# A fused LoRA feed-forward kernel: the first step rebuilt around a table that is split on the chip

## What is computed

```
def _lora_linear(x, W, A, B, adapter_indices):
    base = jnp.einsum('bsd,df->bsf', x, W)
    Ai = A[adapter_indices]
    Bi = B[adapter_indices]
    lora = jnp.einsum('bsr,brf->bsf', jnp.einsum('bsd,bdr->bsr', x, Ai), Bi)
    return base + lora
gate = _lora_linear(x, Wg, Ag, Bg, adapter_indices)
up = _lora_linear(x, Wu, Au, Bu, adapter_indices)
h = jax.nn.silu(gate) * up
x = x + _lora_linear(h, Wd, Ad, Bd, adapter_indices)
w = weights[subjects]                      # subjects: the same numbers
x = x + jnp.einsum('bct,bcd->bdt', x, w)
```

## Time and profile before

| | us |
|---|---|
| median of three runs (1300.89 to 1303.17) | 1301.45 |
| profiled execution | 1302.31 |
| its span | 1300.7 |
| TensorE busy | 1216.8 (94%) |
| VectorE busy | 781.4 (60%) |
| ScalarE busy | 525.4 (40%) |
| GpSimd busy | 94.9 (7%) |

### The profile page before, as it was taken

The page is one execution under the profiler, slowest core; times in us unless marked ns, Lnnn a source line. Parts: engine busy times, 40 slices in busy tenths (PEclk is TensorE's granted clock), DMA queues, the critical chain, the costliest instruction groups (busy, mean ns, idle before and its releaser), DMA issues.

```text
span 1300.7 us, 22988 instructions
## 1 busy us (share of the span) xinstructions
PE 1216.8 (94%) x7104; PEld 1083.9 (83%) x7104; DVE 781.4 (60%) x1389; ACT 525.4 (40%) x999; POOL 94.9 (7%) x188
## 2 busy tenths in 40 slices
PE   3656999989999989999999999998999999999998
PEld 2545778878888878888878888888999999999997
DVE  4534666786667776667777667754444554445453
ACT  2423444454444454344454444434333333334332
POOL 1200110000110000000000000010112111211110
PEclk9777999999999989999999999998999999999999
DMA  3346776477665566757656777656555545554540
GB/s 140 106 144 220 196 211 201 140 207 213 183 180 163 153 187 202 200 151 190 169 160 180 196 212 208 188 167 190 147 168 175 153 142 163 177 151 148 160 131 36
DMA packets 114492, 221.33 MB, mean 170 GB/s; under 512 B 26434, under 2 KB 68546, under 8 KB 114370
## 3 DMA queue, kind: packets, MB, share of 16 engines
q1 hardware_dynamic: 106112, 198.80, 53.0%
q0 software_dynamic: 7392, 19.41, 4.7%
q10 hardware_dynamic: 866, 1.66, 0.3%
HBM read 173.62 MB, written 46.14 MB: 169 GB/s over the span
## 4 chain that ended last, share of the span: by engine, by line
PE 80%; SPq 7%; DVE 4%; issue 3%; DMA 3%; ACT 2%; DVEq 0%; ACTq 0%
PE ps L894 14%; PE ps L895 14%; PE ps L896 13%; PE ps L906 8%; PE ps L1005 5%; PE ps L1009 5%; PE ps L1013 4%; PE ps L1012 4%; PE ps L1007 4%; PE ps L1014 4%; SPq L201 4%; PE ps L923 1%; ACT xo_hi L370 1%; SPq L159 1%; DMA bq<-b_dram 1%
## 5 line engine op out<-in xcount | busy, mean ns | idle before, releaser
L894 PE MATMUL ps<-xo_hi,w_hi 128*128 128x512 f32 x896 | 360.8, 403 | 29.2 <-DVE v L684 13.4
L895 PE MATMUL ps<-xo_lo,w_hi 128*128 128x512 f32 x896 | 356.2, 398 | 0.0
L896 PE MATMUL ps<-xo_hi,w_lo 128*128 128x512 f32 x896 | 353.2, 394 | 0.0
L894 PEld LDWEIGHTS ps<-xo_hi,w_hi 128*128 128x128 f32 x896 | 171.8, 192 | 62.1 <-DVE v L684 16.1
L896 PEld LDWEIGHTS ps<-xo_hi,w_lo 128*128 128x128 f32 x896 | 171.2, 191 | 38.4
L906 PEld LDWEIGHTS ps<-t_st,bq 128*128 128x128 f32 x1024 | 158.1, 191 | 51.2 <-DMA bq<-b_dram 30.9
L895 PEld LDWEIGHTS ps<-xo_lo,w_hi 128*128 128x128 f32 x896 | 171.9, 192 | 26.6
L906 PE MATMUL ps<-t_st,bq 128*128 128x256 f32 x1024 | 165.0, 284 | 28.5 <-DMA bq<-b_dram 28.5
L604 DVE TENSOR_TENSOR w_lo<-wsum,w_hi 128x512 fp32r<-128x512 f32 x128 | 88.5, 692 | 143.7 <-ACT w_hi L370 143.7
L604 DVE TENSOR_TENSOR hl<-h_raw,hh 128x1024 fp32r<-128x1024 f32 x64 | 78.4, 1225 | 158.6 <-ACT hh L370 158.5
L1005 PE MATMUL ps<-wd_hl,hh 128*128 128x320 f32 x512 | 161.5, 315 | 7.5 <-DVE hl L604 4.8
(11 more groups left out here) (73 smaller groups left out, 1559.5 us busy)
## 6 DMA issues: line engine op xcount, KB each, us to landing
bq<-b_dram SPq DMA_DIRECT2D x1024, 64.0 KB, 2.2
raw<-packed SPq DMA_DIRECT2D x64, 512.0 KB, 5.4
h_dram<-h_f SPq DMA_DIRECT2D x64, 512.0 KB, 3.7
h_raw<-h_dram SPq DMA_DIRECT2D x64, 512.0 KB, 4.2
ad_raw<-a_d SPq DMA_DIRECT2D x64, 128.0 KB, 2.8
xs<-x POOLq DMA_DIRECT2D x16, 512.0 KB, 5.1
y_out_dram<-ys POOLq DMA_DIRECT2D x30, 256.0 KB, 3.4
xst<-xg SPq DMA_DIRECT2D x14, 512.0 KB, 6.4
```

What stands on the lines that cost most here:

```text
L894: pe.matmul(bank, st[0], mv[0], start=start and kk == 0, stop=False, skip_group_check=True)
L895: pe.matmul(bank, st[0], mv[1], start=False, stop=False, skip_group_check=True)
L896: m = pe.matmul(bank, st[1], mv[0], start=False, stop=kk == 1, skip_group_check=True)
```

## The change

It rebuilds step 0 and the handling of the table of B:

- The table in HBM is now gathered for the first time unsplit: SP copies for each of the sixteen sequences the raw rows of piece 0 straight from the input into `bq_raw` (two transfers for a slot, `gather_raw`), in the space of the `h_f` buffers. ScalarE (`bq0_hi`) and GpSimd (`bq0_lo`) split them on the chip in two halves, quads 0 and 1, and quads 2 and 3. `make_h2` of the first steps waits for that.
- The split table of the other uses starts with piece 1 and ends with piece 0 (`(i + 1) % PIECES`). Its low part is computed by GpSimd (`b_lo`) and the store is issued by GpSimd (`store_b`) instead of VectorE and SP. The host lays the table out with other axes.
- Four buffers `aq` in group 0, so that `gather_a` doesn't wait for `lora_a`.
- T3 of group 0 is computed by GpSimd; `x_added` is split into one semaphore for each sum.
- Step 0 has its own order on PE (`step_0`), ScalarE and VectorE: A11, A12, then S1, S2, S3, S4, A22 with the four `lora_a` in between, and all four `lora` at the end. The preparation of step 1's weights and the combining of step 0 stand in it too.
- The loads are distributed otherwise: SP loads B11 and B12, ScalarE B21, B22 and then `a_all`. The load of the next weights waits for one more semaphore.

```diff
+X_ORDER = [(B11, B21, T1, T2, T3, B22, NT4)] + [XOPS] * (GROUPS - 1)
...
-        aq = at("aq", 200704, [P, KT * 2, QS, RANK])
+        aq = [at("aq", 200704, [P, KT * 2, QS, RANK])] + [at(f"aq{q}", 186368 + q * 2048, [P, KT * 2, QS, RANK])
+                                                        for q in range(1, QUADS)]
+        bq_raw = at("bq_raw", 139264, [P, QUADS, PIECE, WB])
...
+            def gather_raw(b):
+                slot_numbers[b] = number(sp, b)
+                for half in range(2):
+                    r = half * QR + (b % QS) * RANK
+                    sp.dma_start(bq_raw[r:r + RANK, b // QS, :, :],
+                                 b_gu[0, bass.ds(slot_numbers[b], 1)].rearrange("a r k c -> (a r) k c"))\
+                        .then_inc(bq_raw_in[2 * b // SLOTS], 16)
...
-                sp.wait_ge(b_stored, 16 * (k + 1 if g == 0 else PIECES))
+                sp.wait_ge(b_stored, 16 * (k if g == 0 else PIECES))
...
-            sp.dma_start(xst[B22][:, :], xg[0, :, B22]).then_inc(x_in[B22], 16)
+            sp.dma_start(xst[B12][:, :], xg[0, :, B12]).then_inc(x_in[B12], 16)
             load_w(1)
             sp.wait_ge(idx_in, 16)
-            store_b(0)
-            gather_b(0, 0, SLOTS)
-            for s in range(STEPS):
+            for b in range(SLOTS):
+                gather_raw(b)
+            load_w(2)
+            gather_b(1, 0, SLOTS)
...
-            def load_b(k):
-                pool.wait_ge(b_lo_done, k)
-                pool.dma_start(b_raw[:, :, :], b_gu[k]).then_inc(b_in, 16)
+            def load_b(i):
+                if i:
+                    pool.wait_ge(b_lo_done, i)
+                pool.dma_start(b_raw[:, :, :], b_gu[(i + 1) % PIECES].rearrange("a r k c -> (a r) k c")).then_inc(b_in, 16)
+
+            def b_lo(i):
+                pool.wait_ge(b_hi_done, i + 1)
+                pool.tensor_tensor(b_hl[:, :, WB:2 * WB], b_raw[:, :, :], b_hl[:, :, 0:WB].bitcast(F32), ALU.subtract)\
+                    .then_inc(b_lo_done, 1)
+
+            def store_b(i):
+                pool.wait_ge(b_lo_done, i + 1)
+                pool.dma_start(b_dram[(i + 1) % PIECES].rearrange("a r c -> (a r) c"),
+                               b_hl[:, :, :].bitcast(F32).rearrange("p k c -> p (k c)")).then_inc(b_stored, 16)
+
+            def bq0_lo(pair):
+                q = slice(2 * pair, 2 * pair + 2)
+                pool.wait_ge(bq0_hi_done, pair + 1)
+                pool.tensor_tensor(bq[0][:, q, :, WB:2 * WB], bq_raw[:, q, :, :], bq[0][:, q, :, 0:WB].bitcast(F32),
+                                   ALU.subtract).then_inc(bq0_lo_done, 1)
...
-            pool.dma_start(b_raw[:, :, :], b_gu[0]).then_inc(b_in, 16)
+            load_b(0)
+            pool.wait_ge(x_in[B12], 16)
+            pool.wait_ge(x_in[B22], 16)
+            pool.tensor_tensor(xst[T3][:, :], xst[B22][:, :], xst[B12][:, :], ALU.subtract).then_inc(t3_first, 1)
+            b_lo(0)
+            store_b(0)
...
+            for pair in range(2):
+                bq0_lo(pair)
+            for i in range(1, PIECES):
+                b_lo(i)
+                store_b(i)
+                if i + 1 < PIECES:
+                    load_b(i + 1)
+                if 3 <= i < 7:
+                    gather_a(1, i - 3)
...
+            def bq0_hi(pair):
+                q = slice(2 * pair, 2 * pair + 2)
+                act.wait_ge(bq_raw_in[pair], 16 * SLOTS)
+                hi(bq[0][:, q, :, 0:WB], bq_raw[:, q, :, :]).then_inc(bq0_hi_done, 1)
...
+            x_first(B11)
             w_hi_raw(0)
+            x_first(B21)
+            b_hi(0)
             w_hi_sum(0, 0)
-            x_hi(0, 1)
-            x_hi(0, 2)
-            b_hi(0)
             keep_p1(0)
+            x_first(T1)
+            x_first(T2)
             w_hi_sum(0, 1)
-            for q in range(QUADS):
-                t_hi(0, q)
-                x_hi(0, 3 + q)
+            x_first(T3)
+            x_first(B22)
+            t_hi(0, 0)
+            keep_p5(0)
+            x_first(NT4)
+            t_hi(0, 1)
+            keep_u2(0)
+            w_hi_raw(1)
+            t_hi(0, 2)
+            bq0_hi(0)
+            w_hi_sum(1, 0)
+            t_hi(0, 3)
+            w_hi_sum(1, 1)
+            bq0_hi(1)
+            silu_1(0)
+            silu_2(0)
...
+            x_first(B11)
             w_lo_raw(0)
-            w_add(0, 1)
-            w_add(0, 2)
-            w_add(0, 3)
+            x_first(B21)
+            for k in range(4):
+                w_add(0, k)
+            x_add(0, 1, None)
             w_lo_sum(0, 0)
-            x_add(0, 0, None)
-            x_add(0, 1, None)
-            x_lo(0, 1)
             x_add(0, 2, None)
-            x_lo(0, 2)
-            b_lo(0)
+            x_first(T1)
+            x_first(T2)
             w_lo_sum(0, 1)
             dve.wait_ge(const_in, 48)
-            for q in range(QUADS):
-                t_mask(0, q)
-                if q == 0:
-                    x_add(0, 3, None)
-                t_lo(0, q)
-                x_lo(0, 3 + q)
-            for s in range(STEPS):
+            t_mask(0, 0)
+            x_first(T3)
+            t_lo(0, 0)
+            x_add(0, 3, None)
+            x_first(B22)
+            t_mask(0, 1)
+            x_first(NT4)
+            t_lo(0, 1)
+            for k in range(4):
+                w_add(1, k)
+            w_lo_raw(1)
+            t_mask(0, 2)
+            make_u3(0)
+            t_lo(0, 2)
+            w_lo_sum(1, 0)
+            t_mask(0, 3)
+            t_lo(0, 3)
+            w_lo_sum(1, 1)
+            make_c11(0)
+            make_c22(0)
+            make_c12(0)
...
+            def step_0():
+                def ready(op):
+                    pe.wait_ge(x_lo_done, x_turn(0, XOPS.index(op)) + 1)
+
+                pe.wait_ge(w_lo_done, 1)
+                ready(B11)
+                prod(RA[0], 0, A11, 0, True).then_inc(p1_done, 1)
+                ready(B21)
+                prod(RB[0], 0, A12, 3, True)
+                lora_a(0, 0)
+                lora_a(0, 1)
+                pe.wait_ge(w_lo_done, 2)
+                ready(T1)
+                prod(RC[0], 0, S1, 1, True).then_inc(p5_done, 1)
+                lora_a(0, 2)
+                pe.wait_ge(p1_kept, 1)
+                ready(T2)
+                prod(RA[0], 0, S2, 2, False).then_inc(p6_done, 1)
+                lora_a(0, 3)
+                pe.wait_ge(u2_kept, 1)
+                pe.wait_ge(w_lo_done, 3)
+                ready(T3)
+                prod(RA[0], 0, S3, 4, False).then_inc(p7_done, 1)
+                pe.wait_ge(p5_kept, 1)
+                ready(B22)
+                prod(RC[0], 0, S4, 5, False)
+                pe.wait_ge(u3_done, 1)
+                ready(NT4)
+                prod(RA[0], 0, A22, 6, False)
+                pe.wait_ge(bq0_lo_done, 1)
+                pe.wait_ge(t_lo_done, 4)
+                lora(RB[0], 0, 0, 0, False).then_inc(p2_done, 1)
+                lora(RA[0], 0, 1, 0, False).then_inc(p4_done, 1)
+                pe.wait_ge(bq0_lo_done, 2)
+                pe.wait_ge(t_lo_done, 2 * QUADS)
+                lora(RD, 0, 1, 1, True).then_inc(l22_done, 1)
+                lora(RC[0], 0, 0, 1, False).then_inc(p3_done, 1)
```

More of the change, by code:

```diff
@@ L121, in cond_resid_kernel @@
         w_in = [sem(f"w_in{i}") for i in range(2)]
-        b_in, b_stored = sem("b_in"), sem("b_stored")
+        b_in, b_stored, bq_raw_in = sem("b_in"), sem("b_stored"), [sem(f"bq_raw_in{i}") for i in range(2)]
+        bq0_hi_done, bq0_lo_done = sem("bq0_hi_done"), sem("bq0_lo_done")
         bq_in = [sem(f"bq_in{i}") for i in range(4)]
         h_stored = [sem(f"h_stored{i}") for i in range(2)]
-        x_added, x_hi_done, x_lo_done = sem("x_added"), sem("x_hi_done"), sem("x_lo_done")
+        x_added = {k: sem(f"x_added_{n}") for k, n in ((T1, "t1"), (T2, "t2"), (T3, "t3"), (NT4, "nt4"))}
+        t3_first = sem("t3_first")
+        x_hi_done, x_lo_done = sem("x_hi_done"), sem("x_lo_done")
         w_added, w_hi_done, w_lo_done = sem("w_added"), sem("w_hi_done"), sem("w_lo_done")
@@ L334, in _ @@
             load_b(1)
-            gather_a(1, 0)
-            for k in range(2, 6):
-                load_b(k)
-            gather_a(1, 1)
-            load_b(6)
-            gather_a(1, 2)
-            load_b(7)
-            gather_a(1, 3)
+            for pair in range(2):
[7 more added lines that the diff above has]
+                    gather_a(1, i - 3)
             for g in range(2, GROUPS):
@@ L375, in x_hi @@
                     act.wait_ge(x_in[src], 16 * (g + 1))
+                elif g == 0 and src == T3:
+                    act.wait_ge(t3_first, 1)
                 else:
-                    act.wait_ge(x_added, 4 * g + (T3, T1, T2, NT4).index(src) + 1)
+                    act.wait_ge(x_added[src], g if src == T3 else g + 1)
                 if g:
@@ L516, in x1_split_hi, with x_first @@
                 hi(x1_hi[:, j, :], xs[p % 2][:, j, :]).then_inc(x1_hi_done, 1)
[L518 removed]
```

(26 more changed lines are left out.)

68 lines of the change are left out of this document (27 added, 41 removed).

## The result

Beside each other, the changed kernel takes 1261.28 us (median of four, 1260.81 to 1265.23) and the kernel before 1302.31 (median of four, 1300.89 to 1303.93, one run more than in the table ahead): ratio 0.9688, 95% interval 0.9671 to 0.9704, so 41.0 us or 3.1% faster. The forecast was 1258, range 1249 to 1268.

What follows compares the result with a forecast made beforehand. Late gathers on SP were taken to bound the early steps. Step 15's copy at 46.8 + 4.8 + 2.5 + 0.5 + 168.7 = 223.3 instead of 266.7 saves 43.4 us: 1258 us, range 1249 to 1268.

Steps and rivals of the forecast that it cites:

- Views and bound: Steps 0 to 15: SyncE's store, slot numbers and transfers delay the gathers; 32.9 us lost in steps 2 to 15.
- Raw gather: Step 0, SP: 16 slots take 25.3 us, issues end between 28 and 36, taken as 29; hidden.
- GpSimd's subtractions: Step 0: 2.4 us for 1024 elements; with the copies they push VectorE by 8.4 us.
- VectorE's list: Step 0: 25.1 us of work, taken as the bound; ends at 42.3 instead of 33.9 with GpSimd's push.
- End of step 0: Chain from the fourth mask to eight small products; step 1 starts at 46.8 instead of 60.3, 13.5 us won.
- Four buffers: Step 0, `aq`: GpSimd's waits for PE go; PE idles some 3 us, covered by VectorE, so priced at nothing.
- S2(15): Start of ScalarE's copy of S2's result in step 15: forecast 223.3, before 266.7, so 43.4 us less.
- Clock and first copy: Step 1: low PE clock costs 2.5 us, the wait for the copy of its first product 0.5.
- The light: Rival: GpSimd and VectorE hardly meet or its subtraction is fast; step 1 at 38 to 42, 1249 to 1253; chance 0.12.
- heavy start: Rival: GpSimd subtraction 4 to 5 us or PE at half clock; step 1 at 51 to 56, 1262 to 1268; chance 0.16.
- surviving stall: Rival, steps 0 to 15: gathers still end late, costing 5 to 15 of the 32.9 us; 1263 to 1273; chance 0.10.
- GpSimd's serial chain: Rival: subtractions and stores in series with everything; slower from 15 us for 1024 elements; chance 0.02.

Runs made afterwards that it cites:

- four `aq` alone: The kernel before with only the four buffers for the adapter columns added: 1303.35 us, ratio 0.9990 to 1.0012 to the kernel before.
- A12 late: The changed kernel with TensorE's product A12 of step 0 moved back behind S2 and the last LoRA product: 1261.29 us, ratio 0.9686 to the kernel before.
- x loads later: The changed kernel with the next group's x loaded one step later, behind the second half of gather 2: 1259.05 us, ratio 0.9659 to the kernel before.
- second profile: Profile of the changed kernel run again unchanged, on another comparison's chip: median 1261.13 us, ratio 0.9660 to 0.9695 to the kernel before.
- piece 0 first: The changed kernel with the split table begun with piece 0 and gather 1 in its old place, raw gather kept: 1289.48 us.

## Why the prediction was right, and where it was off

**Views and bound: right.** That the store, the slot numbers and the transfers on SyncE ended step 0, and not the turns of GpSimd and TensorE in front, was read from the releaser at 49.88; the four `aq` alone changed nothing.

**Raw gather: right.** Its issues ended at 28.3; taken was 29.

**GpSimd's subtractions: right. VectorE's list: right in its end by luck.** For GpSimd's own time 2.4, 1.2 and 2.4 us were estimated from a copy, and 2.41, 1.45 and 2.34 came. Each held up VectorE, as forecast: 2.2 + 1.1 + 1.7 = 5.0 us, where 6.0 was taken. The sixteen copies were taken to cost VectorE another 2.4. In the trace its instructions beside them grow by at most 0.09 us each (0.69 to 0.78, 1.22 to 1.31), some 0.5 in all. So the push was 5.5 us and not 8.4. In its place stood something that the sum had at nothing: VectorE idled 4.4 us ahead of the end of its list, 2.17 of it for the first LoRA product. With its start at 8.3 and 24.7 us of work (25.1 taken) the list ended at 42.8, forecast 42.3. A push taken 2.9 us too large and 4.4 us of waits left out nearly cancel.

**End of step 0: 46.8 against 47.37.** The chain was named rightly. Its links in the changed kernel's timeline: the fourth mask ends at 40.54 (40.7 forecast, which rests on the list above), t, weight sums, raw half from 41.98, GpSimd from 43.10 to 45.44 (45.6 forecast), eight products from 45.50. The last took 1.9 us to the next product, 0.7 more than taken, and that is the whole miss: the clock was at its low level of 1.2 GHz until about 50.2. The row taken for their price, at 87.86, holds four products, as the forecast itself says, and the value was not doubled.

**Four buffers: "I price this at nothing" was wrong on two counts.** It was meant for TensorE's new wait for the first copies, 4.80 us in the trace, which VectorE's list was to cover. But VectorE's 2.17 us of idle ahead of the first mask are a wait for the LoRA product behind those copies, so the late copies did reach VectorE. That A12 late cost nothing does not speak against it, since the LoRA products started no later there; what the late copies cost alone no run tells. And I did not price what the kernel would be without the buffers. Once SyncE's chain is gone, GpSimd and TensorE taking turns is the next bound, 9 us away. For the same reason the statement that VectorE's list bounds needs a limit: it bounds only while the copies run ahead.

**Steps 1 to 15: right.** S2(15) was forecast at 223.3 and lies at 224.2 and 223.6. Clock and first copy: S2(1) is 6.15 us behind the start of step 1, where 4.8 + 2.5 + 0.5 = 7.8 was taken, 1.6 too much: the clock was low for 2.8 us of step 1, half of which is 1.4 us and explains the 1.3 above 4.8, and nothing is left for the 0.5 of the first copy. In exchange step 4 waited 1.7 for gather 2, taken as 0, so this sum too is helped by two errors that cancel. (The row of 129 to 130, clock 0.65, puts the end of the low clock there nearer to 129.7 than to the forecast's 129.3; nothing hangs on it.) The forecast had that landing at 86.8 and the need at 87.0; the products came at 87.89. The place was named, and "no reserve at all" was the right reading. With the x loads later the wait is gone.

**The last 2.4 us.** 43.4 were forecast, 41.0 measured in the medians. At step 15 the profiles show 42.6 and 43.2, so some 2 us are lost behind it by the first comparison, where I had written that nothing depends on the change (by the second, 1303.25 to 1261.13, it is 1). The last column of the table shows that stretch: 1035.1 to 1041.1 us over fourteen profiles, with programs that hardly differ behind step 15 (the runs with x loads later differ there in the place of those loads). The changed kernel's first profile took 5.5 us more than before's, its second 1.0. One part varies at the group boundaries: S2(15) to S2(16) is 16.2 us in the profile of before and 18.6 in the changed kernel's first, behind the same 3.13 us of idle TensorE, with the clock at its low level after it in the one with 18.6 and not in the other. But the next boundary is the other way round (18.7 and 17.6), and over all three boundaries it is 52.4 against 53.7 us. The larger part lies behind step 63: 451.9 us to the end in the changed kernel's first profile, 447.7 before and 447.1 to 449.8 in the other profiles. Here it is in windows of 1 us of that first profile (the columns of the earlier trace rows):

```profile
861.00:862.00 1.00, 1.00 (x10) 1.00 (x9) 0.81 (x1) 0.00 (x0) 0.00 (x0) 1.00 0.72 255
...
863.00:864.00 1.00, 0.00 (x0) 0.00 (x0) 0.00 (x0) 0.00 (x0) 0.00 (x0) 1.00 0.61 200
...
866.00:867.00 1.00, 0.59 (x2) 0.59 (x3) 0.49 (x2) 0.53 (x4) 0.00 (x0) 0.50 0.86 242
...
872.00:873.00 1.00, 1.00 (x6) 1.00 (x6) 0.00 (x0) 0.00 (x0) 0.00 (x0) 0.58 0.28 66
```

There TensorE ran the first tiles at full clock, 2.4 GHz, caught up with the loads, waited 4.0 us at 866.41 (1.3 at the same place in the second profile, 0.5 before), and then ran at 1.2 GHz from 866 until about 872.8. This execution is the 1265.23. What decides in which executions the clock falls behind such a gap stays open; I have no runs that vary it alone. That the median difference of 2 us comes from it is an inference from profiles of single executions, not shown.

**Rivals.** The light and the heavy start did not come. The heavy one needed a GpSimd subtraction of 4 to 5 us, or TensorE at half clock through step 0; the subtraction took 2.34, and TensorE's block products stand 0.43 us apart until 15.3 but 0.23 from 27.3 on. The surviving stall did, with 1.7 us at the named place, and only with piece 0 first does it have its full size. GpSimd's serial chain, which would have made the kernel slower from 15 us for 1024 elements on, needed six times the 2.34 measured.

## What to carry to other kernels

Before an edit is priced, take away the wait that ends last and look which one is then next: here the same four buffers were worth nothing behind SyncE's chain and 9 us once that was gone. Most of the gain (28 of 41 us) came from the order in which pieces are prepared: the first one gathered from the raw input, the table started with the piece that is needed next, and that one gathered at once. And give GpSimd a two-input subtraction only where VectorE reads PSUM or waits anyway; back on VectorE the four of step 0 let step 1's mark come 4 us earlier, and 1.6 to 1.9 once the raw halves were split earlier. A forecast that comes out right is worth taking apart: here two sums held because errors of 1.6 to 4.4 us cancelled in them.
